# Diagonal of the attention scores: column sums on TensorE and a ScalarE write, in a fused gated-linear-attention and expert layer

## What is computed

```
q = silu(x @ wq); k = sigmoid(x @ wk); v = x @ wv; f = 1 - k
# per head of 128 channels, two heads, token by token:
S = S * f_t[..., None] + k_t[..., None] * v_t[..., None, :]
o_t = (q_t * scale) @ S            # q and k carry a sign (cos of multiples of pi)
out = layernorm(o * sigmoid(x @ wg1 @ wg2)) * norm_w @ wo
x = x + out
y = x + w2[e] @ relu(w1[e] @ layernorm(x) + b1[e]) + b2[e]     # e = argmax affinity
x = x + alpha * y + (1 - alpha) * x
```

## Time and profile before

| | us |
|---|---|
| median of 3 runs | 679.05 (678.91 to 683.32) |
| the profiled execution, its time | 674.16 |
| its span, first to last instruction | 672.3 |
| one step in the middle of the first part | 37.0 |

### The profile page before, as it was taken

How to read it: one execution, slowest core, us unless ns; L and a number is a source line. 1 busy time by engine, 2 the same in 40 slices (tenths; PEclk the granted TensorE clock), 3 DMA queues, 4 the chain that set the end, 5 groups by cost and what they waited for, 6 DMA issues and landing times.

```text
span 672.3 us, 12520 instructions
## 1 busy us (share of the span) xinstructions
PE 593.8 (88%) x3638; PEld 501.2 (75%) x3639; DVE 343.8 (51%) x864; ACT 280.1 (42%) x671; POOL 226.1 (34%) x384
## 2 busy tenths in 40 slices
PE   3979999999999999977632799999999999999992
PEld 2547676777768677766421799999999999999992
DVE  2395968879595959677147123322322332332331
ACT  3554667575676767552430232223223223223220
POOL 6614262515334351611122122233233233233221
PEclk9999999999999999979665799999999999999997
DMA  9900014141302212020222964455455455455300
GB/s 325 402 12 1 0 33 95 32 94 33 83 12 75 53 32 64 33 63 33 63 63 86 347 232 179 175 217 205 172 203 218 168 202 218 179 189 225 119 29 2
DMA packets 26844, 83.48 MB, mean 124 GB/s; under 512 B 3437, under 2 KB 13039, under 8 KB 20656
## 3 DMA queue, kind: packets, MB, share of 16 engines
q1 hardware_dynamic: 21120, 67.98, 30.4%
q0 software_dynamic: 4992, 14.45, 5.8%
q10 hardware_dynamic: 688, 0.52, 0.2%
HBM read 70.33 MB, written 13.52 MB: 125 GB/s over the span
## 4 chain that ended last, share of the span: by engine, by line
PE 71%; DVE 9%; issue 4%; ACT 2%; POOL 1%; DMA 1%; DVEq 0%; ACTq 0%; POOLq 0%
PE bank_a L1133 21%; PE bank_c L1147 20%; PE bank_l L889 5%; PE bank_a L901 4%; PE bank_c L1003 4%; PE bank_a L930 3%; DVE arena L1198 2%; DVE arena L1209 2%; PE bank_b L981 2%; PE bank_a L946 2%; PE bank_a L939 2%; PE bank_b L980 1%; PE bank_b L1121 1%; PE bank_b L967 1%; PE bank_c L1020 1%
## 5 line engine op out<-in xcount | busy, mean ns | idle before, releaser
L1463 DVE TENSOR_TENSOR arena<-bank_a,b_col 128x512 f32<-128x512 f32 x78 | 54.0, 692 | 189.5 <-PE bank_a L1133 175.7
L1133 PEld LDWEIGHTS bank_a<-masks,arena 128*128 128x128 f32 x1248 | 147.0, 194 | 1.9
L1133 PE MATMUL bank_a<-masks,arena 128*128 128x128 f32 x1248 | 147.1, 277 | 0.0
L1147 PE MATMUL bank_c<-w_sb,arena 128*128 x624 | 141.5, 380 | 1.4 <-ACT arena L864 0.9
L1147 PEld LDWEIGHTS bank_c<-w_sb,arena 128*128 128x128 f32 x624 | 115.5, 190 | 16.4 <-issue 2.3
L889 PEld LDWEIGHTS bank_l<-arena,k_mix 128*128 128x128 f32 x448 | 65.2, 197 | 47.2 <-ACT k_mix L685 34.6
L1198 DVE TENSOR_TENSOR arena<-arena 128x256 f32<-128x256 f32 x224 | 89.6, 442 | 9.3 <-PE bank_l L889 9.3
L864 ACT ACTIVATE arena<-arena 128x512 f32<-128x512 f32 x78 | 45.0, 622 | 107.4 <-PE bank_c L1147 102.9
L889 PE MATMUL bank_l<-arena,k_mix 128*128 128x128 f32 x448 | 72.9, 288 | 14.2 <-DVE arena L1209 12.2
L854 ACT ACTIVATE masks<-bank_b,b_col,g_col 128x128 f32<-128x128 f32 x78 | 31.4, 453 | 129.1 <-PE bank_b L1121 129.1
L901 PE MATMUL bank_a<-arena 128*128 128x512 f32 x160 | 81.9, 611 | 0.0
(11 more groups left out here) (137 smaller groups left out, 747.8 us busy)
## 6 DMA issues: line engine op xcount, KB each, us to landing
arena<-w SPq DMA_DIRECT2D x39, 1024.0 KB
routed_rows<-arena SPq DMA_DIRECT2D x8, 1026.0 KB, 7.8
arena<-x SPq DMA_DIRECT2D x16, 512.0 KB, 5.6
w_sb<-w SPq DMA_DIRECT2D x8, 1024.0 KB, 14.0
arena<-b SPq DMA_DIRECT2D x1, 1024.0 KB, 4.8
arena<-routed_rows,take_now POOLq DMA_INDIRECT x39, 4.1
out<-k_mix,put_now POOLq DMA_INDIRECT x39, 2.5
arena<-wk SPq DMA_DIRECT2D x1, 256.0 KB, 3.9
```

The source lines that it names most:

```text
L1133: m = pe.matmul(bank_a[k // 4][:, k % 4 * P:(k % 4 + 1) * P], w1_now[t.par][:, i * F + k * P:i * F + (k + 1) * P], xl_t[t.par % 2][:, i * ...
L1147: m = pe.matmul(bank_c[p][:, 0:D], h_act[:, k * P:(k + 1) * P], w2_sb[:, bass.ds(e * (FC * D) + k * D, D)], start=(k == 0), stop=(k == FC ...
L1463: dve.tensor_tensor(h_sb[:, n * 512:(n + 1) * 512].rearrange("p (k t) -> p k t", t=P), bank_a[n][:, :].rearrange("p (k t) -> p k t", t=P), ...
```

## The change

The diagonal sums are made as columns. TensorE's `diagonal(a)` runs once a sequence: eight products, one for each chunk, whose stationary side is the chunk of `qk` (128x128) and whose moving side is one column of ones, so that token t's sum lands on partition t, in column n of `bank_a[0]`. They stand between `outputs(b, 0)` and `outputs(b, 1)`. ScalarE's new `attn_diagonal(a)` stands after `mix(a, 0, 1)` and ahead of `rows_of(c)`: it waits for those sums, copies 128x8 of them to `diag_sum`, waits for that copy, and writes eight blocks of 128x128 of `attn_t` as unit matrix times the chunk's column. VectorE's two multiplications are gone, and the transposes of the next step wait for the copy of the sums where they waited for VectorE.

```diff
-                    need(pool, s_dz, H, a, 0)
+                    need(pool, s_dz, 1, a, 0)
...
+            def attn_diagonal(a):
+                need(act, s_dz, 1, a, 1)
+                need(act, s_o, 2, before(a, 2), 2)
+                copy(diag_sum[:, :], bank_a[0][:, 0:NCH]).then_inc(s_sum, 1)
+                need_apart(act, s_sum, 1, a, 1)
+                for n in range(NCH):
+                    act.activation(attn_t[a.par][:, n * P:(n + 1) * P], ident[:, :], ACT.Copy,
+                                   scale=diag_sum[:, n:n + 1]).then_inc(s_at0, 1)
...
                 of(a, mix, 0, 1)
+                of(a, attn_diagonal)
...
             def transposes(a, i):
                 need(pe, s_xn, TJ, a, TJ)
-                need(pe, s_at0, H, a, 0)
+                need(pe, s_sum, 1, a, 0)
...
-            def diagonal(a, h):
+            def diagonal(a):
                 need(pe, s_qk, 1, a, 1)
-                need(pe, s_gate, 2, a, h + 1)
-                pe.matmul(bank_a[1 - h][:, :], ones[:, :], qk[:, h * T:(h + 1) * T], start=True, stop=True).then_inc(s_dz, 1)
+                need(pe, s_gate, 2, a, 2)
+                for n in range(NCH):
+                    m = pe.matmul(bank_a[0][:, n:n + 1], qk[:, n * P:(n + 1) * P], ones[:, 0:1], start=True, stop=True)
+                m.then_inc(s_dz, 1)
...
-                of(a, diagonal, 0)
                 if b is not None:
                     outputs(b, 0, None if c is None else lambda n: affinity(c, n))
-                of(a, diagonal, 1)
+                of(a, diagonal)
                 of(b, outputs, 1)
...
-                    need_apart(dve, s_at0, H, b, H)
+                    need_apart(dve, s_at0, NCH, b, NCH)
...
-            def attn_diagonal(a, h):
-                need(dve, s_o, 2, before(a, 2), 2)
-                need(dve, s_dz, H, a, h + 1)
-                dve.tensor_tensor(attn_t[a.par][:, h * T:(h + 1) * T].rearrange("p (n t) -> p n t", t=P),
-                                  bank_a[1 - h][:, :].rearrange("p (n t) -> p n t", t=P),
-                                  ident[:, :].unsqueeze(1).broadcast_to([P, TJ, P]), ALU.mult).then_inc(s_at0, 1)
```

More of the change, by code:

```diff
@@ L227, in build_program @@
         aff_best = sb("aff_best", [P, TJ], F32)
+        diag_sum = sb("diag_sum", [P, NCH], F32)
         stat = {n: sb(f"{n}_stat", [P, TJ, 6], F32) for n in "xou"}
@@ L287, in build_program @@
         s_dz = sem("diag_summed")
+        s_sum = sem("diag_sums_copied")
         s_at0 = sem("attn_diag_set")
@@ L678, in _ @@
         def _(act):
-            start_at_one(act, [s_mix, s_xn, s_f, s_on, s_xnt, s_k, s_qs, s_g1, s_v, s_gate, s_kt, s_ont, s_x1t, s_alpha, s_zn, s_base, s_xl, s_hr])
+            start_at_one(act, [s_at0, s_sum, s_mix, s_xn, s_f, s_on, s_xnt, s_k, s_qs, s_g1, s_v, s_gate, s_kt, s_ont, s_x1t, s_alpha, s_zn, s_base, s_xl, s_hr])
             act.dma_start(wg1_sb.rearrange("p (c n) -> p c n", c=DC), wg1.rearrange("(c p) n -> p c n", p=P)).then_inc(s_wvg, 16)
@@ L1169, in _ @@
             start_at_one(dve, [*s_stat.values(), *s_mom.values(), s_f0, s_q, s_up, s_pick, s_state, s_og,
-                               s_x1, s_at0, s_aff, s_best, s_hb, s_yb, s_yo])
+                               s_x1, s_aff, s_best, s_hb, s_yb, s_yo])
             def sums(n, src, js):
@@ L1289, in of, with output @@
                         f(s, *args)
-                def output(b, affinities_of=None, diagonal_of=None):
-                    of(diagonal_of, attn_diagonal, 0)
+                def output(b, affinities_of=None):
                     of(b, gating, 0)
@@ L1298, in output @@
                     of(affinities_of, affinities)
-                    of(diagonal_of, attn_diagonal, 1)
                     of(b, gating, 1)
@@ L1350, in step @@
                     centre()
-                output(b, c, a)
+                output(b, c)
                 if b is None:
```

## The result

The changed kernel takes 720.43 us (median of 4 runs, 718.05 to 724.24), the kernel before in the same session 678.98. The ratio is 1.0612, with a 95% interval of 1.0578 to 1.0646: slower by 6.1%, 41.4 us where 33 were forecast. The profiled execution is the longest of the four (724.24; span 722.5), 50.1 above the profiled one of before. Of these 50.1, 2.0 lie ahead of the first changed instruction (the same ScalarE copy starts at 30.09 where it started at 28.05).

What follows compares the result with a forecast made beforehand. TensorE was taken as the bound, busy 35.9 of a 37.00 us step. ScalarE's delay, 21.6, plus the clock, 11.4, gave 33.0 on the median 679.05: 712 us, range 697 to 720.

Steps and rivals of the forecast that it cites:

- The sign: Whole kernel: forecast slower, with chance 0.97; same 0.02, faster 0.01.
- the main term: ScalarE's in-order queue: waiting for the sums and eight writes delay the next step's opening copy; 3.6 us six times, 21.6.
- the upper end of 720: Whole kernel: top of the forecast range from 697 us, just past the forecast with dearer writes.
- VectorE's multiplications, worth nothing: VectorE, each step: sixteen instructions of 0.69 us go, 11.0 in all, but VectorE waits for TensorE there; gain 0.
- TensorE's products, an exchange at par: TensorE's chain at a step's end: 1.82 us removed, eight one-column products of 1.8 added; net 0.
- ScalarE's order, up to the k projection: Step opening: ScalarE waits and writes, its copy starts 3.98 us late, TensorE idles 3.8 before the k projection; 3.6 carried on.
- The sum of 21.6: Six openings with both a and c, each 3.6 us late through ScalarE's queue.
- The clock: TensorE's hole before the k projection: clock falls to 1.2 GHz, losing 1.9 us at six openings, 11.4.
- The failed step: Path after ScalarE's late rows: copy, TensorE's k projection and level, then VectorE's update; 3.6 us an opening carried on.
- ScalarE's order: the main term: Prediction's section on ScalarE's queue: new wait and writes ahead of the rows and opening copy; 3.6 us six times, 21.6.

Runs made afterwards that it cites:

- the last run: Kernel before the change, with the store of c's rows and the following load of x held until the next step's first copy of the transposes; 698.84 us against 679.93.

## Why the prediction was wrong

The sign and the main term were right, the size was not: 41.4 against 33.0, the median at 720.4, past the upper end of 720.

- **VectorE's multiplications, worth nothing: right.** They are gone, and no run shows a gain from it.
- **TensorE's products, an exchange at par: right in time, wrong in effect.** 1.8 us forecast, 1.78 in the chain. But I took the group's cost to be its own length. It brings the clock down behind itself, 13 us where nothing else is changed (691.68 against 678.65).
- **ScalarE's order, up to the k projection: right.** Forecast a wait of 3.35, writes of 0.38 to 0.40 each, a hole of 3.8 and 3.6 us carried on; measured 3.41, 0.386 (median), 3.71, and 3.64 to 3.70 a step. The sum of 21.6 stands beside 23.1 with a clock that holds. Two details differ: the 3.71 is of the run with the load first and 64 columns (in the changed kernel TensorE waits 2.1 at most, since work at the low clock fills the rest), and the k projection waits five times, not six.
- **The clock: right for the hole alone, not in this kernel.** Forecast 11.4 for six falls in the hole; where nothing else brings it down, five cost 9.8. In the changed kernel the hole brings it down at one of the five openings only (at 114.4). The one-column products come first, and most of that low time is hidden, as TensorE has to wait for ScalarE anyway: with the load first, queue and clock together are 25.9, less 22 for the queue about 4. So the term was some 7 us too high here, and by luck made up for nearly half of the one that is missing below.
- **The failed step: the path of the delay, in "ScalarE's order: the main term".** I followed the late rows to the copy and to TensorE, and let everything later hang on VectorE's update. The rows' store waits for them too, and the next x is queued behind that store. SyncE's queue does not appear in the sum; it stood at nothing, without a reason. The lines of before:

```profile
140.72 0.37 SPq L495 DMA_DIRECT2D routed_rows<-arena  x1
141.19 0.44 SPq L486 DMA_DIRECT2D arena<-x  x1
150.40 1.40 DVE L1173 BATCH_NORM_STATS2 x_stat<-arena 128x6 f32<-128x256 f32 x4
```

Counted from the copy of the transposes, the store was issued 1.75 us ahead of it before (140.72 against 142.47) and 0.18 behind it now (158.70 against 158.52): 1.9 us later in the step. Before, x landed 9.0 us after the store's issue (at 149.69), 0.7 ahead of its statistics; now it lands after 10.2 (at 168.87). 1.9 - 0.7 + 1.2 is 2.4 of the wait of 2.74, and VectorE comes to the statistics 0.3 us earlier, counted from the copy. The late x cost 15.5 us, of which the four new waits are 9.0. The second fall of the clock behind each of them fits the rest, but in this kernel that share was not measured apart.

The account of the changed kernel: 22 queue, 4 clock, 15.5 late x with its own fall. That they add up to the measured 41.4 proves nothing: the last two are what is left between two runs (25.9 less 22, and 41.4 less 25.9). Nor are the 4 spread over the steps. The middle ones show none; in the trace of the run with the load first, two openings at which the clock falls a second time (at 113.7 and 277.6) make their steps 1.5 us longer. And the parts are not additive in general: wide products save 9.0 us in the changed kernel (41.4 to 32.4), but cost 7.0 once the load is first (25.9 to 32.9), since the low clock then comes after the hole, in the open, and no longer ahead of it.

Still open is why the pair takes longer where it starts late. From the store's issue to the landing of x it takes 8.7 to 9.6 us in the kernel before, 9.6 to 10.4 in the changed kernel and 9.2 to 10.0 in the last run, in the same order on SyncE.

## What to carry to other kernels

When an instruction is delayed, follow every queue that waits for it, the DMA queues too, and compare each delay with the slack in the trace; here transfers that were ready less than a microsecond early made up over a third of the cost. A wait put into an in-order engine costs the work queued behind it, so place it where that engine already idles. Judge a TensorE instruction by the clock behind it as well as by its length.

## What the runs showed of the hardware

Eight f32 products of 128x128 by one column, 16 records in 1.78 us, let the granted clock fall to 1.2 GHz behind them, though TensorE was busy in every microsecond before; with 64 columns each, in the same arrangement, it stayed at 2.4 GHz through the middle steps. The Trainium skill, page "TensorE: Matmul & The Clock Gate", section "What's actually happening", ties the clock to how busy TensorE has been; by the busy time of the trace these products would have kept it up, and they did not, so here the measurement decides. A low clock can also be free or nearly so: where it falls while TensorE is going to wait for another engine anyway, the middle steps took 40.64 us with the fall and 40.70 without, and 13 us in all went where nothing hid it.
